# The hand-over between the two walks of a graph network kernel: first one-hots of the second walk made earlier, own rows loaded from ScalarE's queue in pieces, a 106-row load cut in two

## The reference, cut to what matters

```python
# layer 0: messages, sums over the destination, GRU cell, residual, layernorm
msg = x[src] + relvectors[edge_type]
red = segment_sum(msg, dst, 6250)
y   = layernorm(x + gru_cell(red, x, w_ih, w_hh, b_ih, b_hh))
# layer 1: symmetric normalised sum over the same edges, residual, layernorm
deg = segment_sum(ones, src, 6250) + 1              # and rsqrt of it
h   = y @ W.T
out = segment_sum(rsqrt(deg)[src] * rsqrt(deg)[dst] * h[dst], src, 6250)   # self loops added again
x2  = layernorm(y + out)
```

## Time and profile before

| what | us |
|---|---|
| median of 3 runs (2242.21 to 2243.59) | 2243.12 |
| the profiled execution, whole | 2245.17 |
| its span, first to last instruction | 2243.3 |
| TensorE busy | 1952.6 (87%) |
| VectorE busy | 1712.7 (76%) |
| GpSimd busy | 1614.3 (72%) |
| ScalarE busy | 908.7 (41%) |

### The profile page before, as it was taken

The page is one execution under the profiler, slowest core; times in us unless marked ns, Lnnn a source line. Parts: engine busy times, 40 slices in busy tenths (PEclk is TensorE's granted clock), DMA queues, the critical chain, the costliest instruction groups (busy, mean ns, idle before and its releaser), DMA issues.

```text
span 2243.3 us, 42544 instructions
## 1 busy us (share of the span) xinstructions
PE 1952.6 (87%) x9408; PEld 1481.1 (66%) x9408; DVE 1712.7 (76%) x3015; ACT 908.7 (41%) x3068; POOL 1614.3 (72%) x1763
## 2 busy tenths in 40 slices
PE   4699887799999999999958998898988898777996
PEld 3477665567777766777736776666766676555885
DVE  5499998899999968888848876677757776444676
ACT  1100000256666634444437874376715776000123
POOL 6777777677777776777644777777777777777772
PEclk8899999899999999999978999999999999999998
DMA  5355555444444456666554333333333333333335
GB/s 148 110 167 174 167 166 165 122 141 141 143 142 143 139 158 185 187 187 180 177 164 141 106 104 106 104 107 104 106 106 104 105 106 106 104 105 105 106 105 154
DMA packets 133915, 302.47 MB, mean 135 GB/s; under 512 B 31024, under 2 KB 67402, under 8 KB 133536
## 3 DMA queue, kind: packets, MB, share of 16 engines
q0 software_dynamic: 79872, 218.21, 34.2%
q10 hardware_dynamic: 37040, 64.87, 8.3%
q1 hardware_dynamic: 16784, 16.78, 2.4%
HBM read 267.74 MB, written 38.40 MB: 136 GB/s over the span
## 4 chain that ended last, share of the span: by engine, by line
POOL 32%; PE 28%; issue 18%; DVE 10%; DMA 5%; DVEq 3%; ACT 1%; SPq 1%; POOLq 0%; ACTq 0%
POOL rows L591 32%; PE ps L1693 16%; PE ps L1889 3%; DMA rows<-gdram,ids 2%; PE ps L1891 2%; DVE sums L896 2%; PE ps L1909 1%; PE ps L1879 1%; DVE sums L959 1%; PE ps L1757 1%; PE ps L1839 1%; DMA sums<-xpd 1%; DVEq L801 1%; DVEq L816 1%; DVEq L813 1%
## 5 line engine op out<-in xcount | busy, mean ns | idle before, releaser
L1693 PE MATMUL ps<-rows,onehot 128*128 x5632 | 1356.8, 394 | 179.6 <-SPq L430 96.7
L1693 PEld LDWEIGHTS ps<-rows,onehot 128*128 128x128 f32 x5632 | 1065.2, 193 | 407.8 <-issue 233.7
L591 POOL DMA_INDIRECT rows<-gdram,ids x832 | 789.2, 949 | 302.8 <-issue 230.3
L591 POOL DMA_INDIRECT rows<-in_x_dram,ids x832 | 798.4, 960 | 271.8 <-issue 240.7
L879 DVE TENSOR_TENSOR sums<-sums,ps 128x256 f32 x400 | 167.4, 418 | 309.2 <-PE ps L1693 296.0
L850 DVE SCALAR_TENSOR_TENSOR onehot<-tkey,node_p,ps 128x512 f32<-128x512 f32 x403 | 298.2, 740 | 9.8 <-issue 6.4
L896 DVE TENSOR_TENSOR sums<-ps,sums 128x800 f16<-128x800 f32 (+1 forms) x156 | 215.4, 1414 | 1.2 <-issue 1.2
L794 DVE SCALAR_TENSOR_TENSOR onehot<-tkey,node_p,ps 128x1024 f32<-128x1024 f32 x152 | 193.3, 1271 | 2.2 <-DVE steps_i L773 1.0
L1465 ACT ACTIVATE wT<-wT,a 128x208 f16<-128x208 f16 x312 | 116.2, 454 | 183.4 <-DVE wT L788 183.4
L1410 ACT COPY sums<-ps 128x256 f32<-128x256 f32 x49 | 18.3, 373 | 350.0 <-PE ps L1749 350.0
L1465 ACT ACTIVATE onehot<-bias,a 128x208 f16<-128x208 f16 x312 | 116.1, 454 | 71.0 <-DVE bias L788 71.0
(11 more groups left out here) (286 smaller groups left out, 2061.5 us busy)
## 6 DMA issues: line engine op xcount, KB each, us to landing
xpd<-sums ACTq DMA_DIRECT2D x48, 384.0 KB, 3.3
sums<-xpd ACTq DMA_DIRECT2D x48, 384.0 KB
rows<-in_x_dram,ids POOLq DMA_INDIRECT x832, 3.0
rows<-gdram,ids POOLq DMA_INDIRECT x832, 2.8
xt<-in_x_dram ACTq DMA_DIRECT2D x96, 128.0 KB, 2.4
gdram<-in_x_dram ACTq DMA_DIRECT2D x5, 1250.0 KB
gdram<-sums ACTq DMA_DIRECT2D x48, 128.0 KB
out_dram<-sums SPq DMA_DIRECT2D x5, 896.0 KB
```

The lines of the kernel that those rows point to most:

```text
L591: pool.indirect_dma_start(rows[:, at:at + D], None, source, bass.IndirectOffsetOnAxis(ap=lists(n, p)[:, s * h + k:s * h + k + 1], axis=0)) ...
L1693: prod = M.matmul(ps[:, h, 0:width], onehot[:, u % U, k, :], rows[:, bass.ds(at + k * stride, width)], start=(k == 0), stop=(k == q - 1))
```

## The change

Three edits:

1. **One-hots.** The one-hots of steps 0 to 2 of the second walk are made by VectorE in node tile 44, between `candidate(44)` and `gates(45)`, and the permission for TensorE's first four steps (`s_acc[1]` raised by U = 4) is given after `gates(48)`, ahead of `blend(47)`. Before, both stood at the start of the second walk.
2. **Own rows.** SyncE no longer loads them. ScalarE issues tiles 0 to 18 in four DMAs of 5, 5, 5 and 4 tiles, behind node tiles 28, 30, 32 and 34 of the first walk, and tiles 19 to 48 in seven DMAs after the last `put_g` and ahead of the first `values`. SyncE goes from the first groups straight to the releases.
3. **Last tile's loads.** Loads of the 106-row tile (x, hidden side, own rows) are cut in 96 and 10 rows. `load_node` now issues the hidden side ahead of x.

```diff
+LAST_PARTS = ((0, LAST // 16 * 16), (LAST // 16 * 16, LAST))
+OWN_FIRST = {28: (0, 5), 30: (5, 5), 32: (10, 5), 34: (15, 4)}
-OWN_B = 1 + -(-(NT - 1 - OWN_A) // FG)
+OWN_B = 2 + -(-(NT - 1 - OWN_A) // FG)
@@ SyncE
-            sp.wait_ge(s_pp, NB + 2)
-            for k in range(2):
-                sp.wait_ge(s_gst[k], (OWN_A + 1 - k) // 2 * 16)
-            own_rows(0, OWN_A // 2, P)
-            own_rows(OWN_A // 2, OWN_A - OWN_A // 2, P)
             first_groups(1, RING1, H1)
-            for k in range(2):
-                sp.wait_ge(s_gst[k], (NT + 1 - k) // 2 * 16)
-            sp.wait_ge(s_x1, NT)
-            sp.wait_ge(s_sums0, 2)
-            for t in range(OWN_A, NT - 1, FG):
-                own_rows(t, min(FG, NT - 1 - t), P)
-            own_rows(NT - 1, 1, LAST)
             groups(1, free1_i, CH * NG1, RING1, H1, CH * J1)
@@ VectorE, walk_second
-                if first == 0:
-                    dve.sem_inc(s_acc[1], U)
+                if first is None:
                     for j in range(U - 1):
                         node_hots(j, j, load(j))
+                    return
@@ VectorE, gates
-                dve.wait_ge(s_gx[k], (t - k) * 16 + 32)
+                dve.wait_ge(s_gx[k], (t - k) * 16 + (64 if t == NT - 1 else 32))
@@ VectorE, node tiles 44 to 48
                 candidate(t, t % 2)
+                if t == J - WIN:
+                    walk_second(None, None)
                 if t < NT - 1:
                     gates(t + 1, (t + 1) % 2)
+                if t == NT - 2:
+                    dve.wait_ge(s_sum_n, NT + 1)
+                    dve.sem_inc(s_acc[1], U)
                 blend(t, t % 2, t % U)
@@ VectorE, ahead of the second walk
-            dve.wait_ge(s_own[0], 2 * 16)
+            dve.wait_ge(s_own[0], len(OWN_FIRST) * 16)
@@ ScalarE, load_node
-                act.dma_start(xt[0:rws, k, :], x[bass.ds(t * P, rws), :]).then_inc(s_gx[k], 16)
-                act.dma_start(xpl[0:rws, k, :], xpd[bass.ds(t * P, rws), :]).then_inc(s_gx[k], 16)
+                for p, z in ((0, P),) if rws == P else LAST_PARTS:
+                    act.dma_start(xpl[p:z, k, :], xpd[t * P + p:t * P + z, :]).then_inc(s_gx[k], 16)
+                    act.dma_start(xt[p:z, k, :], x[t * P + p:t * P + z, :]).then_inc(s_gx[k], 16)
@@ ScalarE, node tiles 4 to 35
-                    node_beside(i * W8 + (U + u), u, i * 2 + u // U)
+                    t = i * W8 + (U + u)
+                    node_beside(t, u, i * 2 + u // U)
+                    if t in OWN_FIRST:
+                        a, tiles = OWN_FIRST[t]
+                        act.wait_ge(s_ext, 1)
+                        for k in range(2):
+                            act.wait_ge(s_gst[k], (a + tiles + 1 - k) // 2 * 16)
+                        own_rows(a, tiles, 0, P, s_own[0])
@@ ScalarE, after the last put_g
+            act.wait_ge(s_x1, NT)
+            act.wait_ge(s_sums0, 2)
+            for k in range(2):
+                act.wait_ge(s_gst[k], (NT + 1 - k) // 2 * 16)
+            for t in range(OWN_A, NT - 1, FG):
+                own_rows(t, min(FG, NT - 1 - t), 0, P, s_own[1])
+            for p, z in LAST_PARTS:
+                own_rows(NT - 1, 1, p, z, s_own[1])
```

More of the change, by code:

```diff
@@ L462, in _ @@
                 sp.sem_inc(s_free[1], 2)
[L464 to L468, removed]
-            sp.wait_ge(s_pp, NB + 2)
-            for k in range(2):
-                sp.wait_ge(s_gst[k], (OWN_A + 1 - k) // 2 * 16)
-            own_rows(0, OWN_A // 2, P)
-            own_rows(OWN_A // 2, OWN_A - OWN_A // 2, P)
-            first_groups(1, RING1, H1)
-            for k in range(2):
-                sp.wait_ge(s_gst[k], (NT + 1 - k) // 2 * 16)
-            sp.wait_ge(s_x1, NT)
-            sp.wait_ge(s_sums0, 2)
-            for t in range(OWN_A, NT - 1, FG):
-                own_rows(t, min(FG, NT - 1 - t), P)
-            own_rows(NT - 1, 1, LAST)
+            first_groups(1, RING1, H1)
             groups(1, free1_i, CH * NG1, RING1, H1, CH * J1)
@@ L840, in walk_second @@
             def walk_second(first, last, task=None, done=None):
-                body = last - first
+                body = last - first if first is not None else 0
                 def load(j):
@@ L1538, in node_beside, with own_rows @@
                 open_gates(t + 1, (u + 1) % 2)
+            def own_rows(t, tiles, p, z, done):
+                act.dma_start(sums1[p:z, t * D:(t + tiles) * D].rearrange("p (s d) -> p s d", d=D),
+                              gdram[t * P + p:t * P + z + (tiles - 1) * P, :].rearrange("(s p) d -> p s d", p=z - p)
+                              ).then_inc(done, 16)
             act.wait_ge(s_acc[0], WIN + 2)
```

## The result

The changed kernel takes 2236.75 us (median of 7 runs, 2233.88 to 2239.63). The kernel before takes 2243.59 us in the same comparison (7 runs, 2242.21 to 2246.87). The ratio is 0.9967, 95% interval 0.9958 to 0.9976: 6.8 us faster, where the prediction had 5.3. The profiled execution spans 2235.6 us against 2243.3.

What follows compares the result with a forecast made beforehand. GpSimd was taken as the bound from its restart on. Span 2243.3 - 5.3 (group 11's gain) = 2238.0, whole 2239.9, median 2.05 below the profiled execution: 2237.8; own range 2234.5 to 2240.5, stated range 2230.5 to 2243.5.

Steps and rivals of the forecast that it cites:

- What bounds: Second walk: after one 48.25 us wait GpSimd never stops, 5.02 us a group, so everything behind moves with its restart.
- Which slots bind: Hand-over to second walk: groups 8, 9 and 10 don't bind; group 11 does, at 1209.6 instead of 1214.95, 5.3 us.
- Tile 48's load: Last node tile: split load lets TensorE end last; 4.45 us at most, `gates(48)` 3.0 us earlier, at 1169.3.
- One-hots beside tile 44: VectorE between `candidate(44)` and `gates(45)`: three one-hots take 4.0 us, 0.7 us lost, bounds 0 and 1.6.
- ScalarE's hold: Seven own-row issues ahead of the first `values` hold ScalarE 9.4 us, 1186.2 to 1195.6; bounds about 3 and 13.
- Own rows in pieces: First walk, own rows of tiles 0 to 18 in four DMAs: cost 0, bounds 0 and 2 us a piece.
- A: Own-row issues before the first `values`: ScalarE isn't held; gain 11.6 us, 2231.5; chance 17%.
- B: Own-row issues before the first `values`: ScalarE held 13 us instead of 9.4; gain 1.7 us, 2241.4; chance 12%.
- C: Tile 48: the split doesn't shorten the load, `gates(48)` at 1173.7; gain 0.9 us, 2242.2; chance 8%.
- D: Tiles 28 to 34: own-row pieces stand before node-tile loads; 17 us lost, 2255; chance 8%.

Runs made afterwards that it cites:

- one lot ahead: Changed kernel, but SyncE issues the seven late own-row loads (tiles 19 to 48) ahead of its releases; 2239.61 us, ratio 0.9976.
- behind two: Changed kernel, but SyncE issues the seven late own-row loads behind its first two releases of the second walk; 2229.69 us, ratio 0.9934.
- one part: Changed kernel with tile 48's load in one part of 106 rows each for hidden side and x; 2239.03 us, ratio 0.9981.
- no late rows: Changed kernel without the own-row loads of tiles 19 to 48, so its result is not the reference's; 2226.48 us, ratio 0.9916.
- the one-hots late: Changed kernel with the three one-hots and the permission back at the second walk's start; ratios 0.995 and 0.9942 on other, slower chips.
- two lots: Changed kernel, late own-row loads on SyncE: three DMAs behind its second release, four behind its third; ratios 0.9914 and 0.9922 on other, slower chips.

## Why the prediction was right, and where it was off

**What bounds.** GpSimd from its restart on, with everything behind it moving along: shown. In the four experiments that ran at 2226 to 2240 us the span less the start of group 11 is 1027.4, 1027.5, 1027.0 and 1027.2 us (in the order one lot ahead, behind two, one part, no late rows), against 1028.35 and 1028.0, while group 11 itself moved by 13.6 us.

**Which slots bind.** Group 11, by step 6, behind a batch behind ScalarE's held queue: shown by the chain after, and by the version without late rows, where group 11 comes 10 us sooner. Groups 8 and 9 were to be free near 1173 and not to bind: group 8 started at 1171.17, and the one-hots late cost 0.3 us at group 11. Group 10 was forecast near 1195 and started at 1192.13.

**Tile 48's load.** 3.0 us forecast for `gates(48)` with edits 1 and 3 together; measured 0.57 + 3.43 = 4.0. The row behind it was right: TensorE ends last, and two more DMA issues delay its start after `gates(47)` by 0.9 us (0.7 forecast). From `gates(47)` to `gates(48)` the forecast was 4.45 - 0.7 = 3.75 us less, and 4.01 were measured. Two terms next to it are off: the one-hots (next paragraph), by 1.3 us, and the 0.58 us that tiles 46 and 47 took longer, which is within what executions differ by. That the second took back part of the first is luck.

**One-hots beside tile 44.** I took 4.0 us and a loss of 0.7. The three stand end to end in 2.40 us, 2.76 with the loads in front, and the place gained 0.57 instead, because the DMA wait they stand in was 3.33. The idle 0.74 us between them before wasn't part of their cost. A gain was outside the bounds that I gave, a loss of 0 to 1.6. That the DMA wait is gone is not the one-hots' doing: with them late, VectorE waits 2.30 to 4.35 us at this place (four profiles), where the profile names a releaser (three of them), for TensorE. The own rows that the first two loads brought at this time before are the likely cause of the old wait; taking them away alone was not tried.

**ScalarE's hold.** 9.4 us forecast, from 1186.2 to 1195.6; measured 8.72, from 1184.78 to 1193.50. It was mainly the second stand that was shorter, 3.10 instead of 3.90. Against this, the hold began 17.9 us after `gates(48)` where I had 16.9: the last store was issued 13.2 us after it instead of 12.4, and ScalarE's first issue follows the end of the store by 0.4 us. `values` 5.85, as taken. Batch and steps 5 and 6 at half clock first: 7.2 us forecast from 1201.5, 7.5 measured from 1199.45 to the copy of indices at 1206.94, SyncE's release included. I had added 0.9 us for the release; here it is within the 7.5. The index copy puts 0.66 us ahead of group 11's first gather after such a wait, which I had left out. So the distance from `gates(48)` to group 11 was forecast 2.35 us shorter than before and is 1.96 shorter: 40.3 against 40.69, with a hold too long and a start too early that nearly cancel.

**Own rows in pieces.** Taken as nothing. From `gates(27)` to `gates(44)`, where the pieces are issued, it is 126.98 us before and 126.97 after, and 126.8 to 127.0 in the four faster experiments, which have the pieces too. The pieces were not tried alone.

**The rivals.** A (no hold) is refuted by the two stands; B (longer hold) by 8.72 us; C by `gates(48)`, which TensorE releases, and by the load in one part, which puts 4.0 us back; D by the unchanged stretch. C's own figure, a gain of 0.9 us, looks too low: the version with the load in one part, which has two DMA issues fewer, gains 2.0 to 6.3. Of the 6.8 us in the medians, the trace accounts for 5.96 as the change's, within the interval of the ratio (5.4 to 9.4 us).

**Slips in the working.** The late own rows are 3.9 MB and not 3.8 (29 tiles of 131 KB and one of 109), which would put 0.3 us on rival B's hold. Four fifths of the forecast's 55% are 44%, not 46%. Neither moves the result.

## What to carry to other kernels

When a queue that holds up the bounding engine is emptied, ask at once what stands behind the work in its new place: the seven DMA issues held either engine for 8.7 to 8.9 us, and what mattered was who was behind them: GpSimd's releases, ScalarE's scalings, or a release that was not due for most of the time. Of the places tried the best was in SyncE's queue behind the two releases that were due early, while the next one still had to wait for TensorE. In two lots no issue stood for 3 us, but that this is faster in total time is not shown. And measure an edit in the company of the others: the one-hots made early were worth 0.3 us at group 11 behind the held queue and 4.4 to 5 us without it.

## What the runs showed of the hardware that I had not expected

The load of the hidden side with 106 rows held VectorE for 10.4 us and landed 10.7 us after its issue, at a DMA share of 0.13. With 96 and 10 rows nobody waited for it. Loads of the same kind with 128 rows, more bytes, landed 3.1 and 3.2 us after their issue where the profile tells it (two in the run behind two releases).

Of own-row DMAs issued in a row, the first three take 0.4 to 0.6 us each. The fourth takes 2.8 to 3.2 us and the fifth 3.1 to 4.5, on SyncE (five profiles) and on ScalarE (four) alike. The first four carry 0.9 MB each, the fifth only 0.13 MB, so it isn't the bytes of a DMA itself that make it stand. When the last four go out 4.8 to 6.2 us after the third, none takes over 0.75 us in three profiles of four, and 1.35 us in the fourth. What the queue runs out of, no run here shows.
